# Between the two edge loops: norm, table store and the table's bf16 parts in two portions instead of one

## The reference

```
x = layernorm(x + L0(x, edge_weight1, src, dst, ...))
x = layernorm(x + L1(x, edge_index, edge_attr_32, ...))
x = layernorm(x + L2(x, layer_weights, edge_weight, edge_index))     # 3 propagation steps
x = layernorm(x + L3(x, edge_weight, src, dst))                      # 10 propagation steps
L0:  m = relu(cat(x[src], x[dst], e) @ W1 + b1) @ W2 + b2;  segment_sum(m, dst)
L1:  msg = relu(x[src] + edge_attr @ We + be);  h = (1 + eps) * x + segment_sum(msg, dst)
     h = relu(h @ W1 + b1) @ W2 + b2; leaky relu; layernorm * gamma + beta
```

## Time and profile before

| | us |
|---|---|
| median of 3 runs | 2695.18 |
| lowest and highest of them | 2695.15 and 2700.47 |
| time of the profiled execution | 2692.2 |
| its span, from the first to the last instruction | 2690.4 |
| mean granted TensorE clock | 0.984 of full speed |
| L0 loop ends, last sum taken over by DVE | 901.18 |
| first gather of the L1 loop starts | 935.09 |

### The profile page before, as it was taken

One profiled execution on the slowest core, in us unless ns is written; L12 is line 12 of the kernel. 1 busy time (PEld: TensorE's weight loads), 2 busy tenths in 40 slices (PEclk: granted clock), 3 DMA queues, 4 the chain that ended last, 5 costly groups with the idle time before them and its releaser, 6 DMA issues.

```text
span 2690.4 us, 59886 instructions
## 1 busy us (share of the span) xinstructions
PE 2607.0 (97%) x18663; PEld 1739.0 (65%) x18663; DVE 1788.8 (66%) x3713; ACT 420.2 (16%) x1080; POOL 1169.4 (43%) x1235
## 2 busy tenths in 40 slices
PE   6899999999999799999999999899999999999998
PEld 5688888888888578888888888533333333333333
DVE  4688888888888599999999999796531111111114
ACT  2122222222222211111111111200100000000001
POOL 4466666666666367777777777200000000000000
PEclk9899999999999799999999999799999999999999
DMA  4222222222222333333333333299999999999997
GB/s 110 52 62 60 60 60 60 61 60 60 59 61 60 61 69 86 77 77 77 78 78 79 78 93 80 83 348 365 341 336 346 351 350 350 351 346 353 359 345 268
DMA packets 376595, 447.32 MB, mean 166 GB/s; under 512 B 154575, under 2 KB 193589, under 8 KB 373290
## 3 DMA queue, kind: packets, MB, share of 16 engines
q1 hardware_dynamic: 323834, 376.76, 43.0%
q0 software_dynamic: 38784, 39.79, 8.0%
q10 hardware_dynamic: 13920, 30.00, 3.0%
HBM read 416.03 MB, written 30.36 MB: 166 GB/s over the span
## 4 chain that ended last, share of the span: by engine, by line
PE 94%; DVE 2%; DMA 1%; ACT 1%; SPq 1%; issue 0%; DVEq 0%; ACTq 0%
PE bank L1577 31%; PE bank L1778 31%; PE bank L1600 11%; PE bank L1589 7%; PE bank L1564 4%; PE bank L1568 3%; PE bank L1749 2%; PE bank L1553 2%; PE bank L1782 1%; DMA arena<-in_edge_weight 1%; SPq L572 0%; PE bank L1736 0%; PE bank L1720 0%; ACT arena L1493 0%; PE bank L1714 0%
## 5 line engine op out<-in xcount | busy, mean ns | idle before, releaser
L1778 PE MATMUL bank<-arena 128*64 128x512 f32 (+1 forms) x4368 | 889.0, 543 | 12.7 <-DVE arena L1087 10.6
L1577 PE MATMUL bank<-arena 128*128 128x320 bf16 x6090 | 882.2, 301 | 8.7 <-DVE arena L840 8.7
L1577 PEld LDWEIGHTS bank<-arena 128*128 128x128 bf16 x6090 | 599.1, 98 | 250.1 <-DVE arena L840 8.9
L658 POOL DMA_INDIRECT arena<-d_p,arena x606 | 573.7, 947 | 299.4 <-issue 240.2
L658 POOL DMA_INDIRECT arena<-d_t,arena x606 | 572.8, 945 | 212.5 <-issue 207.2
L1778 PEld LDWEIGHTS bank<-arena 128*64 128x64 f32 x4368 | 316.2, 136 | 496.7 <-issue 464.3
L1185 DVE TENSOR_TENSOR arena<-bank,arena 128x256 f32<-128x256 f32 (+1 forms) x70 | 27.8, 396 | 572.6 <-PE bank L1749 572.5
L1600 PE MATMUL bank<-arena 128*128 128x150 f32 x2352 | 333.0, 290 | 0.0
L1600 PEld LDWEIGHTS bank<-arena 128*128 128x128 f32 x2352 | 317.8, 189 | 5.3
L847 DVE SCALAR_TENSOR_TENSOR bank<-arena,bank 128x320 f32<-128x320 f32 x404 | 222.7, 552 | 142.5 <-PE bank L1577 142.5
L840 DVE TENSOR_TENSOR arena<-arena,bank 128x1280 bf16<-128x1280 f32 x203 | 299.4, 1475 | 0.0
(11 more groups left out here) (209 smaller groups left out, 1592.9 us busy)
## 6 DMA issues: line engine op xcount, KB each, us to landing
arena<-d_w SPq DMA_DIRECT2D x312, 1024.0 KB, 8.8
arena<-d_code SPq DMA_DIRECT2D x203, 128.0 KB, 3.0
d_w<-arena ACTq DMA_DIRECT2D x24, 1024.0 KB
arena<-in_edge_attr SPq DMA_DIRECT2D x101, 128.0 KB
arena<-d_p,arena POOLq DMA_INDIRECT x606
arena<-d_t,arena POOLq DMA_INDIRECT x606
arena<-d_rec SPq DMA_DIRECT2D x588, 4.0 KB
arena<-d_q SPq DMA_DIRECT2D x202, 11.8 KB
```

The costliest lines, as they stand in the source:

```text
L658: g.indirect_dma_start(G[:, b, j, 0:F], None, table, bass.IndirectOffsetOnAxis(ap=idx[:, b, j:j + 1], axis=0)).then_inc(r.g[b], 16)
L1577: last = t.matmul(psY[g], SOH[:, g, a_, :], X[:, a_, z, :, :], start=a_ == z == 0, stop=a_ == SLICES - 1 and z == PARTS - 1)
L1778: last = t.matmul(banks[t_ % 4][F * (n % 2):F * (n % 2) + F, 0:w_], old[:, n, :], right, start=n < 2, stop=False)
```

## The change

The layer norm between the loops, the table add, the table's store and the making of the three bf16 parts are done in two portions, blocks 0 to 9 and blocks 10 to 24 (`LNP = ((0, 10), (10, 15))`, which was there already for the norm behind L1), and the two are interleaved on DVE and ACT. The `We` loads no longer wait for the table add but only for the memset of `WEBD`; instead SP waits for the whole `xa` (`NB_X1`) before it starts the loop's loads. The `epsn` add stands behind the second portion's variance. The four `roots` ahead of the casts and the three behind are spread: one before the cast of part 1 of the second portion, one and one around the casts of part 2, four at the end. The store is two DMAs, and who waits for it waits for 32 instead of 16. The casts between the loops are counted on `nb_a`, where they were counted on `tab`.

```diff
+NB_X1, NB_TABLE, NB_REST = 21, (16, 22), ((23, 25), (24, 26))
+SQ0, SD0 = (5, 15), (8, 18)
+SQ0_A, SD0_A, CAST_A, NBA_TAB = (1, 3), (2, 5), ((4, 7), (6, 8)), 10
@@ SP
-            sp.wait_ge(s.nb_v, NB_WEBD)
             sp.wait_ge(s.l1z, 3)
             for j in range(4):
                 sp.dma_start(WEBD[ED * j:ED * j + ED, F * j:F * j + F], We).then_inc(s.ld_we, 16)
+            sp.wait_ge(s.nb_v, NB_X1)
@@ POOL
-            pool.wait_ge(s.st_t1, 16)
+            pool.wait_ge(s.st_t1, 32)
@@ DVE
+            beside_x(0)
+            beside_x(1)
+            centre0(0)
+            beside_x(2)
+            variance0(0)
+            beside_x(3)
+            beside_x(4)
+            scaled0(0)
+            centre0(1)
+            table(0)
+            variance0(1)
             v.wait_ge(s.ld_l1, 7 * 16)
             link(d.tensor_scalar(epsn, epsn, 1.0, None, ALU.add))
-            norm(link, s.nb_a, 1, lnA, lnB, lnS, xa)
-            v.wait_ge(s.ld_wts, WTS)
-            link(d.tensor_tensor(lnB, xa, beB.unsqueeze(1).to_broadcast([P, NB, F]), ALU.add))
-            rests(1, lnB, rest1)
-            v.wait_ge(s.tab, 10)
+            scaled0(1)
+            table(1)
+            for z in range(2):
+                for part_ in range(2):
+                    rest_of(part_, z)
+            v.wait_ge(s.nb_a, NBA_TAB)
             v.wait_ge(s.ld_w, 16)
-            v.wait_ge(s.st_t1, 16)
+            v.wait_ge(s.st_t1, 32)
@@ ACT
-            norm(s.nb_v, NB_Y + 4, lnA, lnB, lnS, s.nb_a)
-            act.wait_ge(s.nb_v, NB_X1 + 1)
-            act.dma_start(d_t1.rearrange("(a p) f -> p a f", p=P), lnB).then_inc(s.st_t1, 16)
-            cast(0, lnB)
+            square0(0)
+            root0(0)
+            square0(1)
+            store_table(0)
+            cast1(0, 0)
+            root0(1)
+            store_table(1)
+            cast1(0, 1)
+            cast1(1, 0)
-            roots(0, 4)
-            casts(1, rest1)
-            roots(4, 7)
+            roots(0, 1)
+            cast1(1, 1)
+            roots(1, 2)
+            cast1(2, 0)
+            roots(2, 3)
+            cast1(2, 1)
+            roots(3, 7)
@@ PE
-                pe.wait_ge(s.tab, 5 * layer + 5)
+                pe.wait_ge(s.nb_a if layer else s.tab, NBA_TAB if layer else 5)
```

More of the change, by code:

```diff
@@ L77 @@
 TABW = PARTS * NB * F // 2
-NB_Y, NB_X1, NB_WEBD = 5, 13, 14
+NB_X1, NB_TABLE, NB_REST = 21, (16, 22), ((23, 25), (24, 26))
+SQ0, SD0 = (5, 15), (8, 18)
+SQ0_A, SD0_A, CAST_A, NBA_TAB = (1, 3), (2, 5), ((4, 7), (6, 8)), 10
 ROOTB = (2, 3, 6, 4, 5, 0, 1)
@@ L816, in part, with rests @@
                 return X[:, :, z, :, :].rearrange("p a r f -> p r a f")
-            def rests(layer, whole, rest):
-                v.wait_ge(s.tab, 5 * layer + 1)
+            def rests(whole, rest):
+                v.wait_ge(s.tab, 1)
                 d.tensor_tensor(halves(rest), halves(whole), part(0), ALU.subtract).then_inc(s.tab, 1)
-                v.wait_ge(s.tab, 5 * layer + 3)
+                v.wait_ge(s.tab, 3)
                 d.tensor_tensor(halves(rest), halves(rest), part(1), ALU.subtract).then_inc(s.tab, 1)
-            rests(0, PQ[:, :, 0:F], rest0)
+            rests(PQ[:, :, 0:F], rest0)
             v.wait_ge(s.consts, C_ALL)
@@ L996, in link @@
                 v.wait_ge(s.nb_v, cnt[0])
[L998 to L1008, removed]
@@ L1010, in _, with beside_x, centre0 @@
-            for g5 in range(5):
+            def beside_x(g5):
                 v.wait_ge(s.nb_t, g5 + 1)
-                v.wait_ge(s.ld_x, 16)
                 link(d.tensor_tensor(lnA[:, 5 * g5:5 * g5 + 5, :], banks[g5][:, 0:5 * HALF].rearrange("p (a c) -> p a c", c=HALF)[:, :, 0:F],
                                      xa[:, 5 * g5:5 * g5 + 5, :], ALU.add))
+            def centre0(part_):
+                lo_, n = LNP[part_]
+                y, sc = lnA[:, lo_:lo_ + n, :], lnS[:, :, lo_:lo_ + n]
+                link(d.tensor_reduce(sc[:, 0, :], y, AX, ALU.add))
+                link(d.tensor_scalar(sc[:, 1, :], sc[:, 0, :], -1.0 / F, None, ALU.mult))
+                link(d.tensor_tensor(y, y, sc[:, 1, :].unsqueeze(2).to_broadcast([P, n, F]), ALU.add))
@@ new lines, in variance0, with scaled0 @@
+            def variance0(part_):
+                lo_, n = LNP[part_]
+                sc = lnS[:, :, lo_:lo_ + n]
+                v.wait_ge(s.nb_a, SQ0_A[part_])
+                link(d.tensor_reduce(sc[:, 2, :], lnB[:, lo_:lo_ + n, :], AX, ALU.add))
+                link(d.tensor_scalar(sc[:, 3, :], sc[:, 2, :], 1.0 / F, EPS, ALU.mult, ALU.add))
+            def scaled0(part_):
+                lo_, n = LNP[part_]
+                sc = lnS[:, :, lo_:lo_ + n]
+                v.wait_ge(s.nb_a, SD0_A[part_])
+                link(d.reciprocal(sc[:, 5, :], sc[:, 4, :]))
+                link(d.tensor_tensor(xa[:, lo_:lo_ + n, :], lnA[:, lo_:lo_ + n, :], sc[:, 5, :].unsqueeze(2).to_broadcast([P, n, F]), ALU.mult))
@@ new lines, in table, with rest_of @@
+            def table(part_):
+                lo_, n = LNP[part_]
+                link(d.tensor_tensor(lnB[:, lo_:lo_ + n, :], xa[:, lo_:lo_ + n, :], beB.unsqueeze(1).to_broadcast([P, n, F]), ALU.add))
+            def rest_of(part_, z):
+                lo_, n = LNP[part_]
+                r_ = slice(lo_ // SLICES, (lo_ + n) // SLICES)
+                v.wait_ge(s.nb_a, CAST_A[part_][z])
+                link(d.tensor_tensor(halves(rest1)[:, r_], halves(rest1 if z else lnB)[:, r_], part(z)[:, r_], ALU.subtract))
@@ new lines, in _ @@
+            v.wait_ge(s.ld_x, 16)
+            v.wait_ge(s.ld_wts, WTS)
+            beside_x(0)
+            beside_x(1)
+            centre0(0)
+            assert cnt[0] == SQ0[0]
+            beside_x(2)
+            variance0(0)
+            assert cnt[0] == SD0[0]
+            beside_x(3)
+            beside_x(4)
+            scaled0(0)
+            centre0(1)
+            assert cnt[0] == SQ0[1]
+            table(0)
+            assert cnt[0] == NB_TABLE[0]
+            variance0(1)
+            assert cnt[0] == SD0[1]
@@ L1024, in _ @@
+            for z in range(2):
+                for part_ in range(2):
+                    rest_of(part_, z)
+                    assert cnt[0] == NB_REST[part_][z]
+            v.wait_ge(s.nb_a, NBA_TAB)
             v.wait_ge(s.ld_w, 16)
-            v.wait_ge(s.st_t1, 16)
+            v.wait_ge(s.st_t1, 32)
             def ordered1():
@@ L1308, in _ @@
             a.activation(hiS, banks[5][:, 0:GT * NSB].rearrange("p (z i) -> p z i", z=GT), ACT.Copy).then_inc(s.hi_c, 1)
[L1310 to L1318, removed]
+            act.wait_ge(s.tab, 2)
+            cast(1, rest0)
+            store_q(16, NB)
+            act.wait_ge(s.tab, 4)
+            cast(2, rest0)
             act.wait_ge(s.prep_v, V_DST)
@@ L1362, in quarter_end @@
                               stage[:, q:q + 1, :, :].rearrange("p o a e -> p o (a e)")).then_inc(s.stg[q], 16)
[L1364 to L1368, removed]
             def after(i):
@@ L1416, in _, with square0, root0, store_table @@
             by_order(act, general0, lambda: ordered(0))
-            norm(s.nb_v, NB_Y + 4, lnA, lnB, lnS, s.nb_a)
-            act.wait_ge(s.nb_v, NB_X1 + 1)
-            act.dma_start(d_t1.rearrange("(a p) f -> p a f", p=P), lnB).then_inc(s.st_t1, 16)
-            cast(0, lnB)
+            def square0(part_):
+                lo_, n = LNP[part_]
+                act.wait_ge(s.nb_v, SQ0[part_])
+                a.activation(lnB[:, lo_:lo_ + n, :], lnA[:, lo_:lo_ + n, :], ACT.Square).then_inc(s.nb_a, 1)
+            def root0(part_):
+                lo_, n = LNP[part_]
+                act.wait_ge(s.nb_v, SD0[part_])
+                a.activation(lnS[:, 4, lo_:lo_ + n], lnS[:, 3, lo_:lo_ + n], ACT.Sqrt).then_inc(s.nb_a, 1)
+            def store_table(part_):
+                lo_, n = LNP[part_]
+                act.wait_ge(s.nb_v, NB_TABLE[part_])
+                act.dma_start(d_t1.rearrange("(a p) f -> p a f", p=P)[:, lo_:lo_ + n, :], lnB[:, lo_:lo_ + n, :]).then_inc(s.st_t1, 16)
+            def cast1(z, part_):
+                lo_, n = LNP[part_]
+                act.wait_ge(s.nb_v, NB_REST[part_][z - 1] if z else NB_TABLE[part_])
+                from_ = (rest1 if z else lnB)[:, lo_:lo_ + n, :]
+                a.activation(X[:, :, z, lo_ // SLICES:(lo_ + n) // SLICES, :].rearrange("p a r f -> p r a f"),
+                             from_.rearrange("p (r a) f -> p r a f", a=SLICES), ACT.Copy).then_inc(s.nb_a, 1)
+            square0(0)
[7 more added lines that the diff above has]
+            cast1(1, 0)
             def roots(from_, to):
```

2 lines of the change are left out of this document (1 added, 1 removed).

## The result

| | before | changed |
|---|---|---|
| median, us (15 runs each) | 2695.15 | 2685.51 |
| lowest and highest | 2691.66, 2700.47 | 2683.4, 2693.87 |
| profiled execution | 2692.2 | 2684.23 |
| its span | 2690.4 | 2682.1 |
| L0 loop's last sum starts | 900.98 | 899.54 |

The ratio is 0.9970 with a 95% interval of 0.9961 to 0.9979: 5.7 to 10.5 less. The forecast was 6.8 less and 2688.4, with a range of 2684.0 to 2695.0; the range and the sign hold.

A forecast was written before the change was run, and what follows sets the result against it. PE, busy 97% of the span, bounds the kernel, so only its idle stretches can give time. 3.5 up to xa and 3.4 in the table's parts, less 0.1 for products, give 6.8: 2695.2 to 2688.4, range 2684.0 to 2695.0.

The forecast's parts named there:

- three causes: Up to xa, 3.5 earlier: 1.20 from the wait, 2.3 from the hidden first portion and the overlaps, less the splits.
- the root's table load: ACT's load in the norm, 1.28: hidden behind PE with two fifths of the first half; uncovered they would cost 2.9.
- The parts: Table's parts behind xa: ACT casts one portion while DVE makes the other's rest; 3.4 gained, last cast ends 925.2.
- a sign of being wrong: Between the loops: DVE waiting over 0.5 for a cast of the other portion would show the forecast wrong.
- The gather: First gather of the L1 loop: starts at 928.2, when its one-hot is ready, against 935.09 before.
- priced this at 0 to 0.2: Edge-term products ahead of the first L1 gather: just hidden, at worst costing 0.2; 0.1 was counted.
- The clock: PE's clock in the first L1 gather: between 2.1 less and 2.0 more; nothing counted, both ends kept.
- Rivals 1 and 2: First L1 gather's clock: up, gain 8.9, chance 0.15; low throughout, gain 4.8, chance 0.13 with smaller losses.
- GpSimd: Fetches entering the L1 loop: starts at 925.9 or sooner, 4.2 earlier; slack before the third superblock 2.6, from 5.31.
- Rival 4: GpSimd becomes the L1 loop's bound: fetches 0.03 longer lose 5.3 net, 0.04 longer 11.4 net (2706.6); chance 0.07.
- Splitting's price: Norm and parts between the loops: 0.16 per DVE split, 0.20 per ACT split; some 2 us and 1.5 us added.
- The sum of 6.8: Between the loops: join 6.9 earlier, less 0.1 for the products' worst case by half; forecast chance 0.55.

The follow-up runs named there:

- e1: Kernel before with only the epsn add and its load wait moved behind the variance; last bank add to first gather 24.88, or 24.29 without a pause.
- e2: Changed kernel with only the norm in two portions, table add, store, casts and rests whole; last bank add to first gather 22.35, ratio to before 0.9979.
- e4: Changed kernel with SP loading We only after the whole table add; last bank add to first gather 19.57, ratio to before 0.9990.
- e10: Changed kernel with 24 and 13 filling transposes on PE around the edge-term products; last bank add to first gather 18.87, first gather takes 4.31.
- control: The changed kernel itself, unedited, on the third of the other chips; last bank add to first gather 18.86, ratio to before 0.9994.
- e8: Changed kernel with 4 memsets on GpSimd ahead of its first fetch, 3.1 later; last bank add to first gather 18.85, ratio to before 0.9959.
- e9: Changed kernel with 12 memsets on GpSimd ahead of its first fetch, 9.5 later; last bank add to first gather 18.71, ratio to before 0.9981.
- e13: Changed kernel with 12 memsets on GpSimd ahead of its first fetch, beside the control; last bank add to first gather 18.74, ratio to before 0.9996.
- e3: Changed kernel with the norm whole, only the table's parts in portions; last bank add to first gather 22.34, or 21.77 without a pause.

## Why the prediction was right

- **xa.** Forecast 3.5 earlier by three causes. `xa` ends 8.13 behind the last bank add (916.24 - 908.11), forecast 8.05; two fifths of the norm's first half lie behind PE's W2 products, as said. e1 and e2 measured its terms: 1.35 and 1.94, together 3.29. The prediction counts the root's table load among what is newly hidden, and in that it is wrong: the load had lain beside DVE's variance before. The 3.5 doesn't suffer, since it was taken from the times at which `xa` is ready, not from a price of the load.
- **The parts.** Forecast first one-hot 16.65 behind the last bank add (926.1), measured 16.69. Between the last bank add and the last rest DVE's waits are 0.71 and 0.28 for casts, 0.28 for the square and 0.16 for the root. The 0.71 is over the 0.5 that was named as a sign of being wrong, but it is a wait for a cast of the same portion, and the forecast's own schedule had 0.78 there. The assumption that counted, ACT neighbours overlapping by 0.10, held: three casts and two `roots` from 920.20 to 923.87.
- **The gather** was forecast 18.75 behind the last bank add (928.2), measured 18.86; it is held by its one-hot (1.13 <- line 842). The products started 2.9 ahead of it and were hidden; e4 shows how thin that cover is. I had priced this at 0 to 0.2 and counted 0.1; it was 0, because `We` had been moved.
- **The clock** cost the same as before, 6.32 against 6.42, the value taken. Rivals 1 and 2 didn't come in this execution. The e runs without filling and with both portions gave 5.78 to 6.79, so the 2.1 down and 2.0 up of the range were wider than what was seen, and e10 shows that the lower bound can be had. The Trainium skill, "TensorE: Matmul & The Clock Gate", says in its part on the clock gate that the change of clock falls on other matmuls from run to run; the seven lengths of this gather (5.78, 6.11, 6.23, 6.30, 6.32, 6.62 and 6.79) agree with it, and so do 5.05 and 6.17 for the L0 loop's first gather.
- **GpSimd** started 16.0 behind the last bank add, where 16.5 or less was said, and its slack before the third superblock is 3.35 where 2.6 was reckoned: it started 0.5 sooner, and its first fetch took 0.95 where it had taken 1.22. Rival 4 didn't come.
- **Splitting's price.** The fixed terms of 0.16 and 0.20 came as said (0.83 and 1.16, 0.74 and 1.00). The rule of the Trainium skill, "VectorE: DVE Perf Modes", in its section on the TRN2 errata, that many small tiles pay a fixed latency each, is true here, and it did not decide: ten more DVE instructions added 1.6 of busy time (1788.8 to 1790.4) and the chain got 6.8 shorter. The 1.5 that the prediction reckoned for ACT's five were too much: ACT's busy time grew by 0.6 (420.2 to 420.8).
- **The whole.** The sum of 6.8 met 6.78 in the stretch. To 0.1 that is no luck, since its terms were met one by one; to 0.02 it is, since the 0.1 counted for the products did not come and the gather was 0.11 later than scheduled. The median is another matter: it fell by 9.6, to 2.9 below the forecast, and 6.8 lies in the interval of 5.7 to 10.5; the profiled pair fell by 8.0, 1.4 of it ahead of the change. I had given the scatter of runs 1.5, and the medians differ from the sum by twice that. On the control's chip the same kernel gained 1.9 and not 6.8: the forecast of the whole time holds for the chip that it was made on.

## What to carry to other kernels

When two engines hand whole arrays back and forth on the path, split the array in two so that each works on one half while the other has the other. It costs 0.16 to 0.20 a split here and gave, with the wait of 1.35 that was moved, a quarter of the chain; the first portion can start before the producer is done, and that alone gave 1.94. Then look at what else reads the result: the loads that SP held behind the old end of the chain had to move as well (0.7 if they don't), and a DMA issue left on the busy engine cost 0.43. Measure a gain of 0.25% by the stretch it is in, counted from the last event that both kernels share: it was 18.71 to 18.86 in the five traces (changed kernel, control, e8, e9, e13) that run the same instructions on DVE, ACT and PE, where whole runs scatter by 10. Single instructions that take 0.6 longer than elsewhere (e1, e3) have to be looked for. And look at the stretch behind it too: what is gained ahead of the loop can be lost at its entry.

## What the runs showed of the hardware that was not expected

The same kernel takes 2695 on one chip and 3150 to 3190 on three others, with a mean granted clock of 0.94 to 0.97 there against 0.98. The L1 loop takes 767 on the first and 994 to 1024 on the others. In it PE pauses for about half a us at a time in the middle of groups of matmuls that wait for nothing, and DVE stands in waits for which the profile names no engine of the core ("remote"). The control, from 1300 to 2000 (line waited for, total, times, longest):

```profile
POOL arena L660 <- issue: 304.0, 416, 3.2
...
DVE bank L849 <- remote: 159.6, 54, 3.3
PEld bank L1649 <- issue: 103.0, 133, 2.0
```

On the first chip the L1 loop of the changed kernel has no such row for PE from 937 to 1680, and GpSimd's is the gap between fetches:

```profile
POOL arena L660 <- issue: 184.9, 588, 0.4
```

That the standstill at the loop's entry ends 3.2 to 3.5 behind GpSimd's twelfth fetch ties it to the indirect fetches; how the one holds the other is not shown.
